# A five-pass graph network kernel: 165 chunks instead of 143 fetched row by row on SyncE, 16 rows a step on ScalarE in every layer, a reordered shift, and relation maps on two halves of TensorE's rows

## The reference

```python
# 0: aggr = segment_sum(x[src], dst);  elu((x + aggr) @ W1 + b1) @ W2 + b2
# 1: messages = relu([x[src], x[dst], edge_features] @ mW1 + mb1) @ mW2 + mb2
#    relu([x, segment_sum(messages, dst)] @ uW1 + ub1) @ uW2 + ub2
# 2: h = relu(batch_norm(l2norm(mean_{dst}(x[src]) @ Wl1 + b1 + x @ Wr1)))
#    l2norm(l2norm(mean_{dst}(h[src]) @ Wl2 + b2 + h @ Wr2) + x)
# 3: segment_sum(x[src] @ weight[edge_type], dst), 16 relations of 64 x 64
```

## Time and profile before

| what | before |
|---|---|
| median of 3 runs | 9605.86 us (9603.74 to 9610.63) |
| the profiled execution | 9613.65 us, its span 9611.7 us |
| POOL busy, x7594 instructions | 7166.3 us (75%) |
| PE / DVE / ACT busy | 4955.0 / 2604.7 / 1301.8 us |
| row DMAs of SP, passes 0 to 4 | 3584, 3072, 4096, 3456, 4096 |
| row DMAs of ACT, passes 0 to 4 | 1280, 1536, 3072, 1536, 3072 |
| granted TensorE clock, mean | 0.591 |

### The profile page before, as it was taken

How to read it: one execution, slowest core, us unless ns; L and a number is a source line. 1 busy time by engine, 2 the same in 40 slices (tenths; PEclk the granted TensorE clock), 3 DMA queues, 4 the chain that set the end, 5 groups by cost and what they waited for, 6 DMA issues and landing times.

```text
span 9611.7 us, 127811 instructions
## 1 busy us (share of the span) xinstructions
PE 4955.0 (52%) x23790; PEld 4259.7 (44%) x23791; DVE 2604.7 (27%) x6055; ACT 1301.8 (14%) x2785; POOL 7166.3 (75%) x7594
## 2 busy tenths in 40 slices
PE   4555555566666666344444445666666633333333
PEld 3444444456666665333333334555555522222222
DVE  2222222234444444111121223333333311111111
ACT  1111111111111111000000002222222200000000
POOL 7777777777777777777777777777777667777777
PEclk7555555577777777555555555555555555555555
DMA  3111111133333333111111112222232211111111
GB/s 76 34 34 34 35 34 35 34 93 96 95 94 96 95 95 92 29 31 32 31 32 32 31 31 72 82 83 81 80 84 80 76 32 30 30 30 30 30 30 29
DMA packets 460729, 529.13 MB, mean 55 GB/s; under 512 B 220578, under 2 KB 287616, under 8 KB 459848
## 3 DMA queue, kind: packets, MB, share of 16 engines
q0 software_dynamic: 242880, 349.17, 16.2%
q1 hardware_dynamic: 93785, 88.18, 3.3%
q10 hardware_dynamic: 123247, 83.52, 3.0%
HBM read 442.93 MB, written 77.29 MB: 54 GB/s over the span
## 4 chain that ended last, share of the span: by engine, by line
POOL 70%; issue 23%; PE 3%; ACTq 2%; ACT 1%; DVE 1%; SPq 0%; DMA 0%; POOLq 0%; DVEq 0%
POOL G L520 70%; PE PH L1282 1%; PE PAG L1282 1%; ACTq L383 1%; ACTq L391 1%; PE NA L1282 0%; SPq L422 0%; ACT G L755 0%; PE NB L1282 0%; DVE G L1153 0%; ACT STG L680 0%; ACT Y L663 0%; ACT XT L590 0%; DMA rel_tab<-STG 0%; DVE Y L1038 0%
## 5 line engine op out<-in xcount | busy, mean ns | idle before, releaser
L1282 PE MATMUL PAG<-OH,G 128*64 128x96 f32 (+2 forms) x12126 | 2294.9, 382 | 3742.0 <-DMA G<-rel_tab,IDX 988.0
L1282 PEld LDWEIGHTS PAG<-OH,G 128*64 128x64 f32 (+2 forms) x12126 | 2097.5, 253 | 3971.2 <-issue 3425.2
L520 POOL DMA_INDIRECT G<-rel_tab,IDX x1507 | 1421.9, 944 | 515.7 <-issue 459.6
L520 POOL DMA_INDIRECT G<-far_tab,SRC x1527 | 1440.8, 944 | 485.3 <-issue 465.5
L520 POOL DMA_INDIRECT G<-h_tab,SRC x1524 | 1439.4, 944 | 480.7 <-issue 463.5
L520 POOL DMA_INDIRECT G<-in_x,SRC x1525 | 1440.6, 945 | 475.2 <-issue 464.6
L520 POOL DMA_INDIRECT G<-x_tab,SRC x1507 | 1423.4, 945 | 477.1 <-issue 459.7
L941 DVE TENSOR_TENSOR AGG<-AGG,PAG 64x96 f32 (+2 forms) x980 | 245.8, 251 | 5434.9 <-PE PAG L1282 5432.6
L905 DVE TENSOR_TENSOR OH<-CONST,DREL 128x768 f32<-128x768 f32 x980 | 926.9, 946 | 3.2 <-issue 2.3
L1282 PE MATMUL PAG<-OH,HT 128*128 128x96 f32 x3126 | 615.7, 378 | 583.2 <-ACT HT L748 579.0
L1282 PEld LDWEIGHTS PAG<-OH,HT 128*128 128x128 f32 x3126 | 572.8, 283 | 630.3 <-ACT HT L748 625.3
(11 more groups left out here) (173 smaller groups left out, 3896.4 us busy)
## 6 DMA issues: line engine op xcount, KB each, us to landing
GROWS<-x_tab SPq DMA_DIRECT2D x4096, 0.2 KB
GROWS<-rel_tab SPq DMA_DIRECT2D x4096, 0.2 KB
GROWS<-in_x SPq DMA_DIRECT2D x3584, 0.2 KB
GROWS<-h_tab SPq DMA_DIRECT2D x3456, 0.5 KB
rel_tab<-STG ACTq DMA_DIRECT2D x200, 250.0 KB
GROWS<-far_tab SPq DMA_DIRECT2D x3072, 0.5 KB
GROWS<-x_tab ACTq DMA_DIRECT2D x3072, 0.2 KB
GROWS<-rel_tab ACTq DMA_DIRECT2D x3072, 0.2 KB
```

Source lines behind the costliest of these rows:

```text
L520: pool.indirect_dma_start(out=G[:, h, j, 0:tabs[p].shape[1]], out_offset=None, in_=tabs[p], in_offset=bass.IndirectOffsetOnAxis(ap=numbers ...
L1282: return nc.tensor.matmul(dst, lhsT, rhs, start=start, stop=stop, skip_group_check=True)
```

## The change

- `SP_SUPERS`: 31, 32, 35, 32, 35 chunks in the five passes instead of 28, 24, 32, 27, 32 (165 for 143). Passes 1 and 3 take every sixth super, passes 0, 2 and 4 four supers in 22. In pass 1 the portions of rows are 21 or 22 a super instead of 16.
- `ACT_SUPERS`: every eighth super in all passes: 20, 24, 24, 24, 24 chunks instead of 10, 12, 24, 12, 24 (116 for 82). ACT issues 16 rows a step in all passes, and loads 32 registers at a time instead of 16.
- Pass 3 on DVE: `shift_straight` of super s stands ahead of `add_straight` of super s - 1. PE therefore waits for `added` as well as for `bn_relu` ahead of its sums in pass 3.
- Relation maps: the turned x of the second node half goes to partitions 64 to 127 of `PT` and `XT` (one copy of 128 x 125 instead of 64 x 250), `wrel` is loaded on both partition halves, and the four products are issued as a = 0, a = 1 for b = 0 and then the same for b = 1: those of a = 0 read partitions 0 to 63, those of a = 1 partitions 64 to 127. ACT copies in that order.

```diff
-SP_SUPERS = [range(SHARED + 6, SUPERS - 1, 6), range(8, SUPERS - 1, 8), range(6, SUPERS - 1, 6),
-             [s for s in range(6, SUPERS - 1, 2) if s % 14 in (6, 0)], range(6, SUPERS - 1, 6)]
+EVERY_SIX = list(range(6, SUPERS - 1, 6))
+FOUR_IN_22 = [s for s in range(6, SUPERS - 1, 2) if s % 22 in (6, 12, 18, 0)]
+SP_SUPERS = [[s for s in FOUR_IN_22 if s > SHARED + 2], EVERY_SIX, FOUR_IN_22, EVERY_SIX, FOUR_IN_22]
 ACT_BUFS = 2
-ACT_STEPS = [16, 16, 8, 16, 8]
-ACT_AT_ONCE = 16
+ACT_STEPS = 8
+ACT_AT_ONCE = 32
+ACT_PIECE = P // ACT_STEPS
...
@@ SP, pass 1
-                piece = P // (SP_SUPERS[1][1] - SP_SUPERS[1][0])
+                spacing = SP_SUPERS[1][1] - SP_SUPERS[1][0]
+                ends = [min((s + 1) * P // spacing, P * len(SP_SUPERS[1])) for s in range(SUPERS)]
...
-                    if (s + 1) * piece <= P * len(SP_SUPERS[1]):
-                        some_rows(1, s * piece, (s + 1) * piece)
+                    some_rows(1, ends[s - 1] if s else 0, ends[s])
@@ ACT, node3
-                    flip_copy(3, u)
+                    act.wait_ge(flipped[3], u + 1)
+                    nc.scalar.activation(XT[:, 0:HALF], PT[:, 0:HALF], ACT.Copy).then_inc(flip_copied[3], 1)
...
-                        a, b = k // 2, k % 2
+                        a, b = k % 2, k // 2
@@ DVE, straight
+                        if p == 3:
+                            shift_straight(s, h)
                         if s:
                             add_straight(p, s - 1, starts[s - 1], m)
...
-                        if p == 3:
-                            shift_straight(s, h)
@@ PE, sum_straight
                 elif p == 3:
                     pe.wait_ge(bn_relu, s + 1)
+                    pe.wait_ge(added, SUPERS * p + s + 2)
@@ PE, node3
-                    flip(3, XS, D)
+                    for a in range(2):
+                        last = mm(PT[a * D:(a + 1) * D, 0:HALF], XS[0:HALF, a, :], IDENT[0:HALF, 0:HALF])
+                    last.then_inc(flipped[3], 1)
                     pe.wait_ge(flip_copied[3], u + 1)
-                    for k in range(4):
-                        c = slice(k % 2 * 512, k % 2 * 512 + 512)
-                        mm(PH[k // 2][0:HALF, c], XT[0:D, half(k // 2)], wrel[:, c]).then_inc(l3_map, 1)
+                    for b in range(2):
+                        c = slice(b * 512, b * 512 + 512)
+                        for a in range(2):
+                            k = slice(a * D, (a + 1) * D)
+                            mm(PH[a][0:HALF, c], XT[k, 0:HALF], wrel[k, c]).then_inc(l3_map, 1)
```

More of the change, by code:

```diff
@@ L91 @@
 SHARED = 24
-SP_SUPERS = [range(SHARED + 6, SUPERS - 1, 6), range(8, SUPERS - 1, 8), range(6, SUPERS - 1, 6),
-             [s for s in range(6, SUPERS - 1, 2) if s % 14 in (6, 0)], range(6, SUPERS - 1, 6)]
+EVERY_SIX = list(range(6, SUPERS - 1, 6))
+FOUR_IN_22 = [s for s in range(6, SUPERS - 1, 2) if s % 22 in (6, 12, 18, 0)]
+SP_SUPERS = [[s for s in FOUR_IN_22 if s > SHARED + 2], EVERY_SIX, FOUR_IN_22, EVERY_SIX, FOUR_IN_22]
 ACT_BUFS = 2
-ACT_STEPS = [16, 16, 8, 16, 8]
-ACT_AT_ONCE = 16
+ACT_STEPS = 8
+ACT_AT_ONCE = 32
+ACT_PIECE = P // ACT_STEPS
 ACT_ROWS = SUPERS // 2
-ACT_SUPERS = [range(49 if p == 0 else n + 1, SUPERS - 1, n) for p, n in enumerate(ACT_STEPS)]
+ACT_SUPERS = [range(41, SUPERS - 1, ACT_STEPS)] + [range(ACT_STEPS + 1, SUPERS - 1, ACT_STEPS)] * 4
 def gnn_kernel(nc, x, xT, src_c, src_e, dst_c, dst_r, type_c, type_e, efT, W1, b1, W2, b2, mW1, mb1, mW2T, mb2,
@@ L199, in gnn_kernel @@
         wr2 = sb("wr2", [P, D])
-        wrel = sb("wrel", [D, R * D])
+        wrel = sb("wrel", [2 * D, R * D])
         Z = sb("Z", [P, UNIT])
@@ L205, in gnn_kernel @@
         WARM = sb("WARM", [1, 1])
-        XT = sb("XT", [D + 1, UNIT])
+        XT = sb("XT", [P, UNIT])
         POS = sb("POS", [P, 2 * UNIT])
@@ L322, in gnn_kernel @@
             (ub1c[:, :], ub1), (uw2[:, :], uW2), (wl1[:, :], Wl1), (wr1[:, :], Wr1), (gam[:, :], gamma),
-            (bet[:, :], beta), (wl2[:, :], Wl2), (wr2[:, :], Wr2), (wrel[:, :], Wrel),
+            (bet[:, :], beta), (wl2[:, :], Wl2), (wr2[:, :], Wr2), (wrel[0:D, :], Wrel), (wrel[D:2 * D, :], Wrel),
         ]
@@ L711, in some_rows @@
             def some_rows(p, s, registers, starts):
-                piece = P // ACT_STEPS[p]
-                at = (s + ACT_STEPS[p] + 1 - ACT_SUPERS[p][0]) * piece
+                at = (s + ACT_STEPS + 1 - ACT_SUPERS[p][0]) * ACT_PIECE
                 k, e = at // P, at % P
@@ L725, in some_rows @@
                     starts[:] = row_starts(act, registers, p, ACT_ROWS + ACT_SUPERS[2].index(ACT_SUPERS[p][k]), e)
-                for i in range(piece):
+                for i in range(ACT_PIECE):
                     row(act, p, ROW_BUFS + k % ACT_BUFS, e + i, starts[(at + i) % ACT_AT_ONCE])
@@ L1439, in node1 @@
                     pe.wait_ge(flip_copied[1], u + 1)
-                    mm(NA[:, 0:UNIT], u1[:, :], XT[:, :], stop=False)
+                    mm(NA[:, 0:UNIT], u1[:, :], XT[0:D + 1, :], stop=False)
                     for a in range(2):
```

## The result

The changed kernel takes 10025.26 us (median of 4 runs, 10018.43 to 10032.68) against 9607.27 us (9603.74 to 9610.63): ratio 1.0435, 95% interval 1.0417 to 1.0453. It is 418 us slower; 357 had been forecast (9964 against the 9606 of the prediction). The kernel before was run again beside the experiments, and their ratios are to those runs: median 9624.3 us (9609.82 to 9626.07) beside the first four, 9612.24 us (9606.47 to 9615.81) beside the last four.

The account below looks back on a forecast made before the run. POOL was taken to bound all five passes before the change, ACT pass 3 after it. Terms -16 + 45 - 7 + 339 - 2 = +359 us on 9613.65 gave 9972, as median 9964 us; range 9850 to 10085 us.

Parts of the forecast that it names:

- POOL's price of a gather: On POOL, each chunk fetched by rows instead saves 1.249 us (0.944 + 0.305) while nothing else becomes slower than POOL.
- ACT in pass 3: ACT's unit of four supers grows from 35.6 to 46.3 us against POOL's 38.4, so ACT bounds pass 3: +339 us.
- the load behind the stores: ACT's register load in pass 3, 5.3 us with 16 registers, taken as +1.7 us a unit with 32.
- the lower bound: For ACT's load behind the stores in pass 3: +0.85 us, growing only as an undisturbed load does.
- The maps: Relation maps in pass 3: two products run at once, copies follow at 0.92 us, -2.4 us a unit.
- The rival of the maps one after another: TensorE's two row halves do not work at once in pass 3: unit 48.7 us, 115 more, 10080 us; chance 0.15.
- Shift first: DVE's order in pass 3: removes 2.65 us of waits already left out, so brings nothing more with ACT as bound.
- SP in pass 1: SP's step becomes 10.08 us against POOL's 9.60, making POOL wait after about 45 supers: +45 us instead of -25.
- the last four supers: End of pass 1, streams without rows, each held by the product ahead: about 23 us.
- The rival that SP keeps up by its spare 1.76 us: SP keeps up in pass 1, which gives -25 instead of +45 us: 9894 us; chance 0.13.
- The border behind pass 3: Border between passes 3 and 4: gains about 2 us by the quicker maps.
- The faster rival: POOL still bounds everything, ACT's pass 3 unit at or below 38.4 us: -72, 9534 us; chance 0.05.

Follow-up runs that it names:

- the fitted kernel: Changed kernel with 28 SP chunks in pass 1 (19 rows a super), 18 ACT chunks in pass 3 only in steps without stores: 9533.60 us, ratio 0.9919.
- the maps on one half: Changed kernel with all four relation-map products on the first 64 rows of TensorE and copies in the old order again: 10065.44 us in one run.
- the edits alone: Kernel before, with its old row chunks and 16-register loads, plus shift first and maps on both halves of TensorE's rows: 9595.82 us, ratio 0.9984.
- the load moved: Changed kernel with ACT's load of 32 row addresses in pass 3 moved to the end of the odd step ahead, away from the stores: 9889.45 us.

## Why the prediction was right

**POOL's price of a gather.** 1.249 us held wherever POOL stayed the bound: passes 0, 2 and 4 gave 15, 5 and 3 us for 13, 3 and 3 gathers, and the fitted kernel its 79 us.

**ACT in pass 3.** The main term. The unit was forecast at 46.3 us and lasted 46.77 in the median, the pass was forecast 337 us longer and is 362 longer. The way to it, to take from the unit only the waits that give way when ACT is late and to add everything else, held: in the changed kernel no Relu behind 5900 us waits for more than the issue ahead of it. 16 rows took 5.0 to 5.8 us against the 5.25 taken. The step that was mis-sized is the load behind the stores. It was put at 5.3 + 1.7 = 7.0 us, counted to the first row, and took 7.7 in the median of 48 units (7.0 to 8.8; 7.2 in the unit shown, 6838.88 to 6846.11). It is tied to the next term, which the forecast treated on its own. Against 5.35 in the kernel before, 32 addresses alone (the maps on one half) make 6.2, the quicker copies alone (16 addresses, the edits alone) 6.1, both together 7.7. So 32 addresses by themselves cost the 0.8 us of the lower bound, and the other 1.5 us are what the quicker maps give back. The term was 0.7 us short; over 48 units that is 33 us, enough for the 25 by which the pass came out longer.

**The maps.** That two products run at once was the open point; 3.78 against 7.2 us of PE show that they do, and the copies' distance (0.96 us, forecast 0.92) that ACT then sets the pace. The rival of the maps one after another was priced at 115 us and would have been worth 33 to 40, since the load gives back most of what the copies save. So the saving of 2.4 us a unit was right for the copies and wrong for the unit, 0.4 us. For the changed kernel this is the same error as the 0.7 us above and is not to be counted twice.

**Shift first.** As forecast it is worth nothing once ACT is the bound (6 us in one run, inside the spread).

**SP in pass 1.** +45 us was forecast and +69 measured, the same mechanism in every point: SP does not wait, DVE waits for its streams, POOL for DVE. Two sizes were small. SP's step is 10.14 us and not 10.08, 12 us over 192 supers; most of it is the load, 2.147 us in the median with 2.075 assumed, two in three supers. And the last four supers, put at 23 us, took 34: SP's first stream was at 1923.9 us, 192 steps of 10.145 end at 3871.8, and the last add is at 3905.5. The rival that SP keeps up by its spare 1.76 us fell.

**The border behind pass 3.** The gain of the edits was put at 2 us, from the quicker maps of the last unit. Measured alone it is 16 us (20 in the traces). The step that failed is the view of the border: I priced the last unit's maps and not the arrears of the chain from gather to add, 31.7 us at the last super. The priced part was right: from the last add to the first gather of pass 4 the border is 25.4 us before, 22.8 with the edits alone and 22.4 in the changed kernel. The overlooked part is the other 17 us. POOL hides these arrears as long as it has gathers ahead; they are paid where it has none left. In the changed kernel, where ACT is late through the whole pass, 45.3 us of wait are left instead of 36.7.

**The faster rival.** It needed ACT's unit at 38.4 us or below. Even with the load moved it was 43.9, and POOL waited.

## What to carry to other kernels

An engine that the page shows 14% busy can be full: count the sequencer's time, with the DMA starts and register loads that no busy share holds, and take off only those waits that would vanish if the engine came late. When work is moved from the bounding engine to a helper, divide the helper's free time per round by the price of one piece first; here 19 rows a super fit on SP and 21.3 did not, and 12 a step fit on ACT, kept away from its stores (8 a step did too, beside them), and 16 did not. Where the bounding engine runs out of work, at the end of a pass, it stops hiding the others, so their arrears there are worth as much as its own work.

## What the runs showed of the hardware

- Behind four stores of 250 KB from SBUF, a register load of 32 words took 7.5 us in the median (6.3 to 8.6) instead of 2.15, and 16 row DMAs took 7.6 us to issue instead of 5.3. The faster the stores were issued (copies at 0.96 instead of 1.71 us), the longer the load took (7.5 instead of 6.0 us). A load on SP, which issues none of these stores, took up to 10.3 us beside them.
- Two products of 64 x 125 by 64 x 512 on the two halves of TensorE's rows ran at once, with operands on partitions 0 to 63 and 64 to 127 and the products issued in turn: 3.78 us for four instead of 7.19, both at a granted clock of 0.50.
- A start of a one-row DMA costs its sequencer about 0.33 us (16 in 5.0 to 5.4 us), the same on SP and ACT and for rows of 256 and 512 bytes, as long as it does not stand behind large stores.
- A register load from a table in SBUF took 1.23 us for 16 words and 2.1 to 2.2 us for 32, away from those stores.
